# Delta inputs: the inverses of the first three groups in tensors of their own, and their rows in steps 5 to 8

## The reference, cut to what matters

```python
q, k, v = silu(short_conv(x @ Wq)), ..., ...        # q and k through silu twice; conv over 4 tokens
attn = -(k*beta @ k.T) below the diagonal           # in chunks of 32 tokens, 4 heads
for i in range(1, 32): attn[i, :i] += attn[i] @ attn[:, :i]      # row by row: the inverse
attn += eye;  u = attn @ v;  w = attn @ (k*beta)    # then a scan over the 128 chunks
```

## Time and profile before

| what | us |
|---|---|
| median of 3 runs | 1436.7 |
| the profiled execution, whole | 1436.34 |
| its span, first to last instruction | 1434.6 |
| delta_inputs in it | 606 to 915.3 |
| delta_rule in it | 915.3 to about 1253 |

### The profile page before, as it was taken

One profiled execution on the slowest core, in us unless ns is written; L12 is line 12 of the kernel. 1 busy time (PEld: TensorE's weight loads), 2 busy tenths in 40 slices (PEclk: granted clock), 3 DMA queues, 4 the chain that ended last, 5 costly groups with the idle time before them and its releaser, 6 DMA issues. The chain is left out here.

```text
span 1434.6 us, 36334 instructions
## 1 busy us (share of the span) xinstructions
PE 1277.0 (89%) x12853; PEld 951.4 (66%) x12854; DVE 820.7 (57%) x1882; ACT 463.3 (32%) x1085; POOL 496.5 (35%) x709
## 2 busy tenths in 40 slices
PE   7999999899999999838888887298999999889997
PEld 5888888767776777614554555287888888746565
DVE  6788889533222222248888877457566666435443
ACT  1211222132222222226767774011222222123332
POOL 4344666415411111065666432223343434210000
PEclk9999999889999999968888997558999999779999
DMA  9999910113311211122444434612643334000001
GB/s 309 349 370 340 328 49 31 38 48 109 113 59 60 64 59 59 48 73 95 138 122 119 114 107 136 129 50 74 117 115 89 94 94 147 2 0 30 29 22 37
DMA packets 219962, 156.60 MB, mean 109 GB/s; under 512 B 111744, under 2 KB 201344, under 8 KB 219840
## 3 DMA queue, kind: packets, MB, share of 16 engines
q1 hardware_dynamic: 204288, 129.11, 30.7%
q0 software_dynamic: 9312, 25.44, 5.4%
q10 hardware_dynamic: 6240, 0.39, 0.3%
HBM read 64.47 MB, written 90.44 MB: 108 GB/s over the span
## 5 line engine op out<-in xcount | busy, mean ns | idle before, releaser
L945 PE MATMUL ps_sc<-w,a_qeo 128*128 x568 | 183.1, 466 | 0.0
L753 DVE TENSOR_TENSOR a_stm<-a_vpad,ps_sc 128x352 f32<-128x352 f32 x71 | 37.0, 521 | 177.2 <-ACT a_vpad L517 177.2
L945 PEld LDWEIGHTS ps_sc<-w,a_qeo 128*128 128x128 f32 x568 | 104.0, 193 | 46.5 <-issue 2.5
L423 POOL DMA_DIRECT2D x_slots<-a_stm x66 | 36.4, 551 | 226.1 <-issue 226.1
L1585 PE MATMUL d_pp<-d_xT,d_w_p 128*128 128x512 f32 x192 | 112.1, 732 | 1.1 <-ACT d_xT L1320 1.1
L1477 DVE SCALAR_TENSOR_TENSOR d_cout<-d_cin,d_taps,d_cout 128x512 f32<-128x512 f32 x144 | 106.1, 747 | 6.1 <-ACT d_cout L1338 2.7
L915 PE MATMUL ps_kv<-w,a_stm 128*128 x426 | 105.7, 384 | 1.2 <-DVE a_stm L746 1.1
L915 PEld LDWEIGHTS ps_kv<-w,a_stm 128*128 128x128 f32 x426 | 79.2, 190 | 30.1 <-issue 12.5
L2328 PE MATMUL g_pp<-g_xT,g_w_g 128*128 128x512 f32 x192 | 90.8, 613 | 8.3 <-ACT g_xT L2219 8.3
L1253 POOL DMA_INDIRECT got<-x_slots,d_idx x64 | 75.5, 1180 | 18.7 <-issue 16.1
L517 ACT ACTIVATE a_vpad<-ps_sc 128x352 f32<-128x352 f32 x71 | 33.0, 464 | 140.0 <-PE ps_sc L945 140.0
(11 more groups left out here) (273 smaller groups left out, 2834.4 us busy)
## 6 DMA issues: line engine op xcount, KB each, us to landing
x_slots<-a_zeros SPq DMA_DIRECT2D x32, 1024.0 KB, 11.0
rec<-d_kve SPq DMA_DIRECT2D x32, 384.0 KB, 2.9
u_kve<-rec SPq DMA_DIRECT2D x32, 384.0 KB, 3.9
a_qeo<-x_slots SPq DMA_DIRECT2D x71, 128.0 KB, 2.0
x_slots<-a_stm POOLq DMA_DIRECT2D x66, 128.0 KB, 2.1
rec<-d_act_out SPq DMA_DIRECT2D x32, 256.0 KB, 3.7
u_qkT<-rec SPq DMA_DIRECT2D x32, 256.0 KB, 3.5
w<-in_w SPq DMA_DIRECT2D x4, 1408.0 KB, 14.0
```

The lines of the kernel that those rows point to most:

```text
L753: dve.tensor_tensor(e_h[:, q, 0:HID], e_gate[:, q, :], ps_3[q], ALU.mult).then_inc(h_out, 1)
L945: mm = pe.matmul(ps, e_xT[:, q, k, :], w13[:, s, k, bass.ds(e_hidden, 1), :], start=(k == 0), stop=(k == KD - 1))
```

## The change

The inverses of the first three groups and their products get tensors of their own. POOL clears them right behind the first gather, ahead of the four small clearings that DVE and PE wait for at the start. The rows move to steps 5 to 8, into the place between L1509 and L1513. SP sends all twelve DMAs of inverses at the top of its step 9, ahead of the last group's records; ACT sends none. POOL's clearing of `t_out` in step 8 stays, for `delta_rule`.

```diff
+EARLY_ROWS_AT = {5: (1, 8), 6: (8, 11), 7: (11, 13), 8: (13, SUB)}
-        prod = xn[:, :, :, :].rearrange("p q j (b c) -> p (q j) b c", c=SUB)
+        t_early = sb("t_early", [P, PART[1], SUB, 2, SUB])
+        prod = sb("prod", [P, PART[1], SUB, SUB])
 # SP, in step(i, par), first thing
+                if i == NG + 1:
+                    sp.wait_ge(sub_done, 1)
+                    for g in range(PART[1]):
+                        for s in range(2):
+                            send_inverses(sp, t_early, t_mat, g, s, t_sent[0])
 # SP, behind the steps
-            sp.wait_ge(sub_done, 1)
-            for u in range(PART[1]):
-                send_inverses(sp, t_out, t_mat, u, 0, t_sent[0])
 # POOL
             gather(0, 0, (0, 1, 2, 3))
+            pool.memset(t_early[:, :, :, :, :], 0.0).then_inc(early_unit, 1)
             pool.memset(power[:, :, 0, :], -0.5).then_inc(zeroed, 1)
...
             pool.wait_ge(zeroed, 4)
+            pool.wait_ge(early_unit, 1)
+            pool.memset(t_early.rearrange("p g i z c -> p g (i z c)")[:, :, 0:2 * SUB * SUB:2 * SUB + 1], 1.0).then_inc(early_unit, 1)
 # ACT, behind the steps
-            act.wait_ge(sub_done, 1)
-            for u in range(PART[1]):
-                send_inverses(act, t_out, t_mat, u, 1, t_sent[0])
 # DVE
                 if lo == 1:
-                    dve.wait_ge(unit, 2)
-                    dve.wait_ge(p_done, USES * (NG - 1) + 2)
+                    dve.wait_ge(early_unit, 2)
                     dve.wait_ge(l_back[0], 16 * 2 * PART[1])
-                inverse_rows(dve, t_out, l_in, prod, sub_own, 0, lo, hi)
+                inverse_rows(dve, t_early, l_in, prod, sub_own, 0, lo, hi)
...
-                if i == NG:
-                    rows(1, 7)          # behind conv(5)
+                if i in EARLY_ROWS_AT:
+                    rows(*EARLY_ROWS_AT[i])    # between L1509 and L1513
-                if i == NG:
-                    rows(7, 11)         # behind conv(2)
-                if i == NG + 1:
-                    rows(11, SUB)
```

More of the change, by code:

```diff
@@ L1197, in delta_inputs @@
         unit = sem("unit")
+        early_unit = sem("early_unit")
         sub_own = sem("sub_own")
@@ L1434, in rows @@
                 if lo == 1:
-                    dve.wait_ge(unit, 2)
-                    dve.wait_ge(p_done, USES * (NG - 1) + 2)
+                    dve.wait_ge(early_unit, 2)
                     dve.wait_ge(l_back[0], 16 * 2 * PART[1])
-                inverse_rows(dve, t_out, l_in, prod, sub_own, 0, lo, hi)
+                inverse_rows(dve, t_early, l_in, prod, sub_own, 0, lo, hi)
                 if hi == SUB:
                     dve.wait_ge(sub_own, 30)
-                    dve.tensor_copy(t_out[:, 0:PART[1], :, 1, :],
-                                    t_out[:, 0:PART[1], :, 0, :].rearrange("p g i c -> p g c i")).then_inc(sub_done, 1)
+                    dve.tensor_copy(t_early[:, :, :, 1, :], t_early[:, :, :, 0, :].rearrange("p g i c -> p g c i")).then_inc(sub_done, 1)
             def add_experts(i, par, j):
```

## The result

The changed kernel takes 1430.3 us (median of 9 runs, 1422.2 to 1432.4) against 1437.9 us (9 runs, 1433.1 to 1441.7): ratio 0.9942, 95% interval 0.9930 to 0.9954, so 8.3 us less (6.6 to 10.1). A second set of six runs (experiment 11) gave 0.9943 (0.9921 to 0.9964). The forecast was 1427, 9.6 us less.

A forecast was written before the change was run, and what follows sets the result against it. DVE sets a step's length except for a 3.87 us hole, and SP's chain bounds the border. Terms +1.4, +0.2, -0.35 and -10.9 sum to -9.6: 1436.3 to 1426.7, said as 1427, own range 1422 to 1431, wider range 1420 to 1434.

The forecast's parts named there:

- The start, plus 1.4: At the start: POOL's new clearing of 1536 elements delays DVE and everything behind it by 1.38 us, bounds 0.5 to 3.5.
- Rows 8 to 12 in steps 6 and 7, nothing: Steps 6 and 7: the rows take 3.06 and 2.96 us, fit DVE's 3.87 us wait for `dec`, and cost nothing.
- Rows 1 to 7 in step 5, plus 0.2: Step 5: 3.7 us of rows fit the 3.87 us hole; a late read-back may cost 0 to 1 us, 0.2 taken.
- the 1 us more that I had worked out from the rule: Steps 5 and 8: by the skill's shared-port rule rows 7 and 15 wait for `dec`, about 1 us more; not added.
- Step 8, minus 0.35: Step 8: 3.5 us of rows stick out of the hole, 3.85 leave the place behind `conv(2)`; bounds -0.35 and -3.2.
- The border, minus 10.9: Border of the blocks: earlier sums and moved sends start the next block at 904.4 instead of 915.3; gain 9.4 to 13.8 us.
- POOL's root ends at 900.8, just inside: Border, quick end: POOL's last root finishes at 900.8, before SP's chain lets the next block begin at 901.5.
- 0.3 for the barrier: Border: 0.3 us added between the end of SP's chain and the start of the next block.
- The sends did not become the bound: Rival at the border: twelve slow sends on SP take the gain, 1430 to 1439 us, most near 1432; chance 0.12.
- The hole is a hole: Rival in steps 5 to 8: DVE's rows delay ACT or POOL for `dec`, so they cost in full, 1440 us; chance 0.06.
- the only large one: In a full step: DVE's 3.87 us wait for POOL's `dec` before L1513 is its only large hole.
- The clock did not change by a whole tile: Rival in the scans: the number of tiles at TensorE's low clock changes, 4.4 us each; chance 0.12, 0.04 beyond two tiles.

The follow-up runs named there:

- experiment 11: The changed kernel again, unaltered, on the chip of the two runs with POOL's last root halved or left out: 1428.3 us against 1434.9, ratio 0.9943.
- experiment 2: Kernel before with three clearings of 1536 elements of a spare tensor ahead of the four small ones: 1443.6 us against 1438.7, ratio 1.0032.
- experiments 4: Changed kernel with rows shifted by one, so no product stands beside POOL's `dec` in steps 5 to 7: ratio 0.9960 to the kernel before.
- experiment 8: Kernel before with one more POOL operation of `dec`'s size (1024 elements, SBUF to SBUF) in each of the eight tails: ratio 1.0088, 12.7 us more.
- experiment 7: Changed kernel with the clearing late, SP's twelve sends in step 8, and rows 13 and 14 behind conv(5): 1422.6 us against 1439.3, ratio 0.9875.
- experiment 3: Changed kernel with the sends back behind the ten steps, six on ACT's queue and six on SP's: ratio 0.9983 to the kernel before.
- experiments 9 to 11: 9, 10: experiment 7's kernel with POOL's last root halved (ratio 0.9905) or left out (0.9868); experiment 11 has its own line.
- experiment 1: Changed kernel with the two clearings of the new tensor moved on POOL to the end of its step 3: ratio 0.9944 to the kernel before.
- experiments 5 to 8: 5: changed kernel, clearing late, sends in step 8, ratio 0.9924; 6: changed kernel without the twelve sends, 0.9944; experiment 7 and experiment 8 have own lines.

## Why the prediction was right, and which step failed

**The start, plus 1.4: right.** The clearing took 1.40 us, DVE began 1.3 us later behind the first gather, and experiment 2 shows that a late start reaches the end.

**Rows 8 to 12 in steps 6 and 7, nothing: right.** 0.77 and 0.99 us of the hole are left.

**Rows 1 to 7 in step 5, plus 0.2: a little too low, for a wrong reason.** They cost about 0.55 us, since `dec` held row 7's product for 0.75. I had read from the earlier trace rows that the port is not shared: the convolutions ran at 751 ns beside POOL's 5.44 us root. But the root works on 32 elements in 5.4 us, and `dec` on 1024 in 1.05. The Trainium skill (SBUF — State Buffer, "SBUF: two separate sides") has a VectorE operation with two SBUF inputs wait for the whole of a GpSimd operation that reads SBUF. For `dec` and row 7 the trace agrees, and experiments 4 and 8 show the hold from both sides. For the root it doesn't, in the kernel before (its root began at 875.73):
```profile
875.97 0.17 DVE L1537 TENSOR_TENSOR small<-d_beta,d_over 128x16 f32<-128x16 f32 x1
```
This is the very product that experiment 8's operation held. What sets the root apart is not shown. Row 15, which by the rule would have waited for `dec` too, took 1.32 us against 1.30 before: it began 0.09 us ahead of `dec`'s end. So the measured cost lies between my 0.2 and the 1 us more that I had worked out from the rule.

**Step 8, minus 0.35: right** (-0.1 in the profiles), with the wait in front of L1508 longer as forecast. What the prediction did not see is that this longer wait could hold rows too; that is experiment 7's 3.2 us.

**The border, minus 10.9: this is the step that failed**, in its size and in its mechanism. The prediction put it as "POOL's root ends at 900.8, just inside", with "0.3 for the barrier", and let SP's queue decide between 9.4 and 13.8 us. Measured are 9.2. On SP, twelve sends took 10.0 us (forecast 8.6 to 11.7) and the eight records 7.0 (forecast 4.6); the chain ended 29.0 us behind step 8's sums, within the 25.7 to 30.1 drawn. But POOL's chain was later: 0.27 us behind the sums the root begins, it takes 5.43, the two small operations about 0.45, and from POOL's last instruction to the next block it takes 5.55 us in every trace where nothing else is later. Together 11.7 us behind the sums of step 9, unless SP ends later still, as in experiment 3. In the kernel before POOL waited 10.06 us there, because SP's landing was later; a stretch of 5.55 us could not be seen in it. With 11.7 behind sums that come at 894.9 plus what steps add, the term would have been 8.8 us and the forecast 1429. The forecast came near the measured 1430.3 without luck: the four terms as measured, 1.3, 0.55, -0.1 and -9.2, add to -7.4 us, and the runs say -6.6 to -10.1.

**The rivals.** The sends did not become the bound. The hole is a hole. But it isn't "the only large one", as the prediction called it: the wait for ACT ahead of L1508, 0.3 to 3.2 us in steps 3 to 7 of the traces here, is the second, and the length of a step goes with it. The clock did not change by a whole tile: before and after, L2065 (now L2063) takes 2.08 us in the first four tiles and once more further on, at the same place.

```profile
982.25 1.16 PE L2063 MATMUL u_bank_g<-u_qkT 64*128 64x128 f32 x16
996.45 2.08 PE L2063 MATMUL u_bank_g<-u_qkT 64*128 64x128 f32 x16
1009.93 1.16 PE L2063 MATMUL u_bank_g<-u_qkT 64*128 64x128 f32 x16
1019.11 1.16 PE L2063 MATMUL u_bank_g<-u_qkT 64*128 64x128 f32 x16
```
The tile that begins with 2.08 us is again 13.5 us long and its neighbour 9.2, as in the earlier trace rows.

**The 5 us in steps 0 to 7 and the 3 in the rest** are not shown to be the change's, but for the 0.55. The kernel before with three clearings has the long steps, the changed kernel has 160.9 and 157.7 us in two executions, and its scans with the last layer 516.2 and 518.9. What is longer is DVE's wait for ACT ahead of L1508: over steps 3 to 7 of twelve traces (all but experiment 8's) it and the length of the step correlate at 0.96. Why ACT comes late there stays open. Two things go with it. One is the chip: all three traces of the chip of experiments 9 to 11 have 157.0 to 158.0 us in steps 3 to 7, the seven of experiments 1 to 7, on two others, 160.7 to 163.0, and the kernel before takes 1434.9 us on the first and 1438.7 and 1439.3 on the others. The chip of the first two profiles isn't on record, and the kernel before was profiled unchanged only once. The other is TensorE's clock: over the 35 runs of the kernel before on one chip, time and mean granted clock correlate at -0.84 (clock 0.920 in the mean), and the 12 of experiment 1 at -0.97, but the 11 runs of the kernel before beside experiments 5 to 8 only at -0.34. Step by step, over the same 60 steps, length and granted clock correlate at -0.17, so the clock of a step doesn't tell its length. The profiled execution of before was, at 1436.3, below its kernel's median of 1437.9, so part of what looks lost in the comparison of two traces had never been there to lose.

## What to carry to other kernels

At a barrier between two blocks, list for every engine its last instruction and what its queue needs behind it; the one with the late finish need not be the one with the long visible queue, and a cost can lie hidden in a wait that something else ends. Before trusting that two engines don't disturb each other, look for a pair of the same kind, streaming the same number of elements, not for the longest operation that happens to overlap. When the difference of two profiled executions holds stretches that the change does not touch, profile either kernel a second time, on the same chip, before explaining them.

## What the runs showed of the hardware

- POOL's last instruction to the first of the next block: 5.55 us in seven kernels where nothing else was later. When POOL had ended 18 us earlier, the next block began 0.65 us behind SP's last issue. What POOL does there was not tried.
- POOL's power took 5.43 us for 32 elements per partition, 2.90 for 16 and 1.01 to 1.53 for 4.
- A DVE product with two SBUF inputs is held until a POOL operation of 1024 elements from SBUF has ended: 16 elements 1.52 or 0.83 us instead of 0.17, 147 elements 1.16 instead of 0.41. Beside POOL's power of 32 elements (5.4 us) the same 16 elements took 0.17.
- Six sends of 64 KB in short pieces took 5.0 us on ACT's queue beside SP's `l32` writes and 10.5 beside its 2.6 MB of records.
